# Thirteen of 64 gathered columns of an edge stage looked up by one-hot matmuls

## The reference

```
a_src = (h * att_src).sum(-1);  a_dst = (h * att_dst).sum(-1)
e     = leaky_relu(a_src[src] + a_dst[dst], 0.2)
ee    = exp(e - segment_max(e, dst)[dst])
agg   = segment_sum(h[src] * ee / segment_sum(ee, dst)[dst], dst)
```

## Time and profile before

| | us |
|---|---|
| median of 3 runs (10355.76 to 10371.48) | 10368.38 |
| profiled execution | 10367.71 |
| its span | 10366.0 |
| busy: PE / DVE / ACT / POOL | 4951.9 / 4237.3 / 2175.2 / 5594.5 |
| edge stage, from its first DMA to its last scan | 4590 to 9754 |

### The profile page before, as it was taken

One profiled execution on the slowest core, in us unless ns is written; L12 is line 12 of the kernel. 1 busy time (PEld: TensorE's weight loads), 2 busy tenths in 40 slices (PEclk: granted clock), 3 DMA queues, 4 the chain that ended last, 5 costly groups with the idle time before them and its releaser, 6 DMA issues. The chain is left out here.

```text
span 10366.0 us, 77502 instructions
## 1 busy us (share of the span) xinstructions
PE 4951.9 (48%) x21339; PEld 2907.9 (28%) x21339; DVE 4237.3 (41%) x9137; ACT 2175.2 (21%) x4107; POOL 5594.5 (54%) x5263
## 2 busy tenths in 40 slices
PE   6888888779955888841221112111221112111145
PEld 5555655557742344410010001000000001000011
DVE  5666566556669877731111111111111111111188
ACT  3443444323311222211111111111111111111000
POOL 2333333300013456357777777777777777777652
PEclk9898888889977999965565556655565556555577
DMA  2000000021110222231111111111111111111455
GB/s 91 34 28 33 25 24 25 22 85 61 57 63 25 55 52 53 38 73 35 37 40 35 34 35 39 38 35 34 38 40 34 35 36 38 39 34 35 69 181 186
DMA packets 388197, 510.48 MB, mean 49 GB/s; under 512 B 216517, under 2 KB 303358, under 8 KB 365442
## 3 DMA queue, kind: packets, MB, share of 16 engines
q1 hardware_dynamic: 191618, 258.32, 8.7%
q0 software_dynamic: 163968, 75.75, 6.5%
q10 hardware_dynamic: 32256, 171.98, 4.1%
HBM read 245.58 MB, written 263.86 MB: 49 GB/s over the span
## 5 line engine op out<-in xcount | busy, mean ns | idle before, releaser
L1665 POOL DMA_INDIRECT e_row<-rows_dram,e_idx x4096 | 3890.3, 950 | 1264.1 <-issue 1248.2
L1610 PE MATMUL e_bank<-e_hid,e_w 128*128 128x512 f32 x1024 | 592.6, 714 | 4050.7 <-ACT e_hid L1640 4050.7
L1698 DVE COPY e_idx<-e_allidx 128x64 int32 x64 | 13.6, 212 | 4205.1 <-DMA e_row<-rows_dram,e_idx 4205.1
L1610 PEld LDWEIGHTS e_bank<-e_hid,e_w 128*128 128x128 f32 x1024 | 220.8, 223 | 4353.7 <-issue 4353.7
L387 POOL COPY a_xc<-a_xp 128x1573 f32<-128x1573 f32 x104 | 400.3, 3853 | 679.5 <-PE a_bank L441 563.9
L1648 ACT ACTIVATE e_ex<-e_dx 128x512 f32<-128x512 f32 x64 | 38.5, 602 | 3418.1 <-DVEq L1711 3418.1
L1047 POOL DMA_INDIRECT c_yt<-yb_dram,keep_slots x256 | 384.6, 1502 | 580.3 <-DVE c_yg L1267 501.0
L396 POOL DMA_INDIRECT xb_dram<-a_so,a_sidx x256 | 251.9, 984 | 744.9 <-DVE a_sidx L669 416.8
L1603 PE MATMUL e_bank<-e_h,e_w 128*128 128x512 f32 x1024 | 509.8, 627 | 76.3 <-DMA e_h<-hn_dram 76.3
L199 DVE TENSOR_TENSOR a_cnta_hot<-a_cnta_iota,a_cnta_part 128x512 bf16<-128x512 bf16 x1184 | 518.0, 438 | 0.0
L1168 PE MATMUL c_conv<-c_xp,c_w 128*128 128x512 f32 x1152 | 513.7, 600 | 0.0
(11 more groups left out here) (353 smaller groups left out, 10090.5 us busy)
## 6 DMA issues: line engine op xcount, KB each, us to landing
e_row<-rows_dram,e_idx POOLq DMA_INDIRECT x4096
ys_dram<-e_y ACTq DMA_DIRECT2D x64, 1024.0 KB, 3.9
f_ye<-ys_dram SPq DMA_DIRECT2D x64, 1024.0 KB, 4.8
res_dram<-e_st ACTq DMA_DIRECT2D x64, 768.0 KB, 3.3
xb_dram<-a_taps SPq DMA_DIRECT2D x4, 5120.0 KB, 31.1
b_tok<-xb_dram SPq DMA_DIRECT2D x80, 256.0 KB, 2.6
yb_dram<-b_y ACTq DMA_DIRECT2D x80, 256.0 KB, 2.0
x_dram<-a_xs SPq DMA_DIRECT2D x9, 2048.0 KB, 6.3
```

The costliest lines, as they stand in the source:

```text
L1610: mm = nc.tensor.matmul(bank[UPB + n % DNB][:], w2[:, n % NE, f], hid[:, n % 2, f], start=(f == 0), stop=(f == NF1 - 1))
L1665: nc.gpsimd.indirect_dma_start(row[:, s, u], None, rows, bass.IndirectOffsetOnAxis(ap=idx[:, s, u:u + 1], axis=0)).then_inc(gath[s], 16)
```

## The change

Of each chunk's 64 columns POOL gathers the first 51 (UP); the other 13 (XG) are looked up by TensorE. A node index is split into a low part (10 bits: 8 groups g of 128) and a high part (5 bits: 32). The feature table of all nodes, 16 values each, lies in SBUF: partition l, group g, 32 x 16 values, 16 KB per partition. It is held as two pieces in float32r, a type of fewer mantissa bits: the rounded table, and what the rounding left; both products add in float32 in PSUM.

One look-up k (one column, 128 edges): PE multiplies a matrix whose columns all are the column's low codes with the identity, so that every partition has all 128 codes (`spread`); DVE compares them with 8 x 128 constants and gets 8 one-hot weights (`one_hot`); PE multiplies these with the 2 x 8 pieces and accumulates 16 matmuls of 512 columns into one bank (`found`): for each edge 32 candidates of 16 features; DVE multiplies them by a mask of the high code (`pick`) and sums over the 32. After 13 of them DVE computes the attention sums of these columns.

One-hots and `found` exist twice, `spread` once. DVE makes the one-hot of look-up k + 2 right after the product of look-up k. PE's order per chunk is look-ups 0 and 1, the experts, look-ups 2 to 12. ACT now does the experts of the next chunk before the exponentials of this one. `up` has two PSUM banks (the others go to `found` and `spread`). DVE waits for a stored state one use of the buffer later. The block before clears the first experts' semaphores on ACT. The indices have a semaphore of their own, so POOL doesn't wait for the weights; the table comes in by eight DMAs ahead of them on SP.

```diff
-    U = 64
+def edge_states(nc, passed, rows, srcs, cont, v, res, hn, ys, ident, att_src, w):
+
+
+    U, XG = 64, 13
+    UP = U - XG
     TURNS = FE // (2 * U)
-    UPB, DNB = 4, 2
+    CHUNKS = 2 * TURNS
+    UPB, DNB = 2, 2
+    HG, HS, PARTS = 8, NHI // 8, 2
...
+        codei = sb("codei", [P, 2, CHUNKS + 1, XG], I32)
+        code = sb("code", [P, 2, XG])
+        high = sb("high", [P, XG])
+        lowi, lows = sb("lowi", [P, HG], I32), sb("lows", [P, HG])
+        highi, highs = sb("highi", [P, HS], I32), sb("highs", [P, HS])
+        table = sb("table", [P, HG, HS, HF])
+        pieces = sb("pieces", [P, PARTS, HG, HS, HF], mybir.dt.float32r)
+        att = sb("att", [P, HF])
+        hot = sb("hot", [P, 2, HG, P], mybir.dt.float32r)
+        pick = sb("pick", [P, XG, HS])
+        prod = sb("prod", [P, 2, HS, HF])
+        aprod = sb("aprod", [P, XG, HF])
...
+        spread = ps("spread", [P, P])
+        found = [ps(f"found{z}", [P, HS, HF]) for z in range(2)]
+        bank = [ps(f"bank{i}", [P, NT]) for i in range(UPB + DNB)]
...
+        table_g = rows.rearrange("(s g l) c -> g l s c", g=HG, l=P)
...
-            sp.dma_start(allidx[:, 0:FE], srcs).then_inc(consts, 16)
+            sp.dma_start(allidx[:, 0:FE], srcs).then_inc(listed, 16)
+            for g in range(HG):
+                sp.dma_start(table[:, g], table_g[g][:, :, 0:HF]).then_inc(tabled, 16)
             for dst, src in ((w1[:], w["w1"].rearrange("e d f -> d e f")),
                              (w2[:], w["w2"].rearrange("e (f p) d -> p e f d", p=P)),
-                             (b1[:], w["b1"]), (b2[:], w["b2"])):
+                             (b1[:], w["b1"]), (b2[:], w["b2"]), (att[:], att_src.broadcast_to([P, HF]))):
...
+            def spread_code(k):
+                s, j = divmod(k % (2 * XG), XG)
+                nc.tensor.matmul(spread[:], code[:, s, j:j + 1].broadcast_to([P, P]), ident[:], start=True,
+                                 stop=True).then_inc(code_spread, 1)
+
             pe.wait_ge(consts, 80)
+            pe.wait_ge(coded, 1)
+            spread_code(0)
+            pe.wait_ge(pieced, 2 * PARTS - 1)
             with pe.Fori(0, TURNS) as i:
+                def look_up(k):
+                    pe.wait_ge(hot_ready, 2 * XG * i + (k + 1))
+                    spread_code(k + 1)
+                    pe.wait_ge(masked, 2 * XG * i + (k + 1))
+                    for g in range(HG):
+                        for q in range(PARTS):
+                            mm = nc.tensor.matmul(found[k % 2][:].rearrange("p s c -> p (s c)"), hot[:, k % 2, g],
+                                                  pieces[:, q, g].rearrange("p s c -> p (s c)"),
+                                                  start=(g == 0 and q == 0), stop=(g == HG - 1 and q == PARTS - 1))
+                    mm.then_inc(found_psum, 1)
...
-                up(0)
-                for n in range(TURN):
-                    if n + 1 < TURN:
-                        up(n + 1)
-                    down(n)
+                for s in range(2):
+                    for j in range(2):
+                        look_up(XG * s + j)
+                    up(STEP * s)
+                    for n in range(STEP * s, STEP * (s + 1)):
+                        if n + 1 < STEP * (s + 1):
+                            up(n + 1)
+                        down(n)
+                    for j in range(2, XG):
+                        look_up(XG * s + j)
+            pe.wait_ge(hot_ready, XG * CHUNKS + 1)
+            spread_code(1)
...
+            def experts_of(i, s):
...
+                outputs((s + 1) * STEP - 1)
+                act.wait_ge(y_ready, DNB + TURN * i + (s + 1) * STEP)
+                act.dma_start(ys[2 * i + s], y[:, s]).then_inc(y_stored[s], 16)
+
+            def states_of(i, s):
+                act.wait_ge(dx_ready, 2 * i + s + 1)
+                nc.scalar.activation(ex[:], dx[:], ACT.Exp)
+                nc.scalar.activation(weight[:], dx[:, 1], ACT.Exp).then_inc(ex_ready, 1)
+                act.wait_ge(st_ready, 2 * i + s + 1)
+                act.dma_start(res_c[2 * i + s], st[:, s]).then_inc(stored[s], 16)
+
+            experts_of(0, 0)
+            with act.Fori(0, TURNS - 1) as i:
+                experts_of(i, 1)
+                states_of(i, 0)
+                experts_of(i + 1, 0)
+                states_of(i, 1)
+            experts_of(TURNS - 1, 1)
             for s in range(2):
-                act.wait_ge(stored[s], 16 * TURNS)
+                states_of(TURNS - 1, s)
...
-                    for u in range(U):
+                    for u in range(UP):
...
+            dve.wait_ge(listed, 16)
+            for s in range(2):
+                nc.vector.tensor_copy(idx[:, s], allidx[:, s * U:s * U + UP]).then_inc(idx_ready, 1)
+            looked_up = allidx[:, 0:FE].rearrange("p (n u) -> p n u", u=U)[:, :, UP:]
+            nc.vector.tensor_scalar(codei[:, 0, 0:CHUNKS], looked_up, HG * P - 1, None, ALU.bitwise_and)
+            nc.vector.tensor_scalar(codei[:, 1, 0:CHUNKS], looked_up, (HG * P).bit_length() - 1, None,
+                                    ALU.logical_shift_right).then_inc(init, 1)
+            dve.wait_ge(made, 2)
+            nc.vector.tensor_copy(lows[:], lowi[:])
+            nc.vector.tensor_copy(highs[:], highi[:])
+            dve.wait_ge(init, 2)
+            nc.vector.tensor_copy(code[:, 0], codei[:, 0, 0]).then_inc(coded, 1)
+            dve.wait_ge(coded, 1)
             dve.wait_ge(consts, 80)
-            for s in range(2):
-                nc.vector.tensor_copy(idx[:, s], allidx[:, s * U:(s + 1) * U]).then_inc(idx_ready, 1)
-            dve.wait_ge(init, 1)
-            K = 13
+
+            def one_hot(k, first):
+                dve.wait_ge(code_spread, first + (k + 1))
+                nc.vector.tensor_tensor(hot[:, k % 2], spread[:].unsqueeze(1).broadcast_to([P, HG, P]),
+                                        lows[:].unsqueeze(2).broadcast_to([P, HG, P]), ALU.is_equal
+                                        ).then_inc(hot_ready, 1)
+
+            one_hot(0, 0)
+            dve.wait_ge(tabled, 16 * HG)
+            for q in range(PARTS):
+                nc.vector.tensor_copy(pieces[:, q], table[:]).then_inc(pieced, 1)
+                if q < PARTS - 1:
+                    dve.wait_ge(pieced, 2 * q + 1)
+                    nc.vector.tensor_tensor(table[:], table[:], pieces[:, q], ALU.subtract).then_inc(pieced, 1)
+                    dve.wait_ge(pieced, 2 * q + 2)
+            one_hot(1, 0)
+            K = 18
             with dve.Fori(0, TURNS) as i:
                 for s in range(2):
                     n = 2 * i + s
                     link = Chain(dve, chain, K * n)
+                    link(nc.vector.tensor_copy(code[:, 1 - s], codei[:, 0, bass.ds(n + 1, 1)].rearrange(
+                        "p n u -> p (n u)")))
+                    link(nc.vector.tensor_copy(high[:], codei[:, 1, bass.ds(n, 1)].rearrange("p n u -> p (n u)")))
+                    link(nc.vector.tensor_tensor(pick[:], highs[:].unsqueeze(1).broadcast_to([P, XG, HS]),
+                                                 high[:].unsqueeze(2).broadcast_to([P, XG, HS]), ALU.is_equal))
+                    for j in range(XG):
+                        k = XG * s + j
+                        dve.wait_ge(found_psum, 2 * XG * i + (k + 1))
+                        nc.vector.tensor_tensor(prod[:, k % 2], found[k % 2][:],
+                                                pick[:, j].unsqueeze(2).broadcast_to([P, HS, HF]), ALU.mult
+                                                ).then_inc(masked, 1)
+                        one_hot(k + 2, 2 * XG * i)
+                        dve.wait_ge(masked, 2 * XG * i + (k + 3))
+                        nc.vector.tensor_reduce(row[:, s, UP + j, 0:HF], prod[:, k % 2].rearrange("p s c -> p c s"),
+                                                AX.X, ALU.add).then_inc(picked, 1)
+                    dve.wait_ge(picked, 2 * XG * i + XG * (s + 1))
+                    link(nc.vector.tensor_tensor(aprod[:], row[:, s, UP:, 0:HF],
+                                                 att[:].unsqueeze(1).broadcast_to([P, XG, HF]), ALU.mult))
+                    link(nc.vector.tensor_reduce(row[:, s, UP:, HF:],
+                                                 aprod[:].rearrange("p u (h e) -> p u h e", e=NE), AX.X, ALU.add))
...
-                    dve.wait_ge(gath[s], 16 * U * i + 16 * U)
-
-                    nc.vector.tensor_copy(idx[:, s], allidx[:, bass.ds((2 * i + s + 2) * U, U)]
+                    dve.wait_ge(gath[s], 16 * UP * i + 16 * UP)
+
+                    nc.vector.tensor_copy(idx[:, s], allidx[:, bass.ds((2 * i + s + 2) * U, UP)]
...
+                    dve.wait_ge(stored[s], 16 * i + 16)
...
-                for s in range(2):
-                    dve.wait_ge(stored[s], 16 * i + 16)
```

More of the change, by code:

```diff
@@ L1487, in _ @@
             sp.wait_ge(fixed, 16)
+        @block.scalar
+        def _(act):
```

(38 more changed lines are left out.)

22 lines of the change are left out of this document (14 added, 8 removed).

## The result

The changed kernel takes 10,502.5 us (median of 4 runs, 10,498.3 to 10,504.6) against 10,369.4 (median of 4 runs): by the ratio of the means 1.0131 times as long, 95% interval 1.0113 to 1.0148. The forecast was 10,235, faster; its sign was wrong. The profiled execution took 10,503.91 us, its span 10,502.1.

A forecast was written before the change was run, and what follows sets the result against it. GpSimd's gathers were taken to set the 80.3 us chunk period. Afterwards a loop through four engines sums to 77.6 us; 63 periods plus start and end give 133 us less, 10,235 us, range 10,050 to 10,620.

The forecast's parts named there:

- the price of one matmul: TensorE's look-up: a 512-column float32r matmul takes 0.214 us, the lower end of 0.214 to 0.857.
- T: Edge stage: the period of one chunk, 80.3 us before the change and forecast at 77.6 after it.
- The experts and the order of waits: Edge stage: experts 13.85 us; then exponentials, states and the other 11 look-ups follow one another, once per chunk.
- The pause: TensorE stands still once per chunk during exponentials, states and the next one-hot: 13.3 us.
- the slow clock: TensorE restarts at the lower of two clock levels after standing still, costing 2.45 us per chunk.
- hand-overs: Edge stage: waits not visible in a row, 0.3 us per chunk, bounds 0 and 2.
- The terms of the start: Edge stage: constants at 47 us, preparation, two cold look-ups, experts, eleven look-ups; first chunk's last look-up 124 us in.
- The turning point: Edge stage: the gain is gone at a period of 79.7 us, 10 ns more for each of 208 matmuls.
- C: Look-ups: VectorE sets the pace (10,610 us) or hand-overs are longer (10,340); with other periods of 80 to 85, chance 0.17.
- B: Look-up matmuls: float32r moves at half the rate, 0.429 us each, time 13,100 us; chance 0.11.
- A: Edge stage: GpSimd's gathers stay the bound at 64.0 us per chunk, time 9,323 us; chance 0.07.
- D: TensorE keeps its clock through the pause: 75.2 us per chunk, 10,080 us; chance included in the forecast's 0.58.

## Why the prediction was wrong

*The step that failed* is the price of one matmul: "float32r keeps fewer bits than float32 (hence two pieces), so it needs no second half-word pass and lies nearest to the bf16 row. The look-up is 0.24 + 16 x 0.214 = 3.66 us, and 13 are 47.6." The second pass is indeed gone (13,312 records for as many matmuls), but a float32r matmul takes 0.2333 us, not 0.214. The look-up is 3.96 us, thirteen are 51.5. That is 3.9 us per chunk and 245 of the 269 us by which the profiled execution missed; the kernel with two bf16 pieces, which has the forecast's look-up, has the forecast's time.

*The other terms of T.* The experts and the order of waits came as forecast. The pause is 13.54 (forecast 13.3), the slow clock 2.77 (2.45), what is left for hand-overs 0.24 (0.3). DVE needs 0.691 + 1.214 + 1.020 = 2.93 us a look-up (3.25) and waits 1.2 in each in the mean. The constants landed at 4631, 39 us in (47); the first chunk's last look-up was done at 4712.3 (4714), and the other 63 took 81.85 each: 9868.8. (The terms of the start add up to 123 us, not to the 124 used.)

*The turning point* was named: the gain gone at 10 ns a matmul more. It was 19 ns more. But the step took the lower end of 0.214 to 0.857 for a type of which the earlier trace rows held none, and gave all that lay above it 0.28: 0.17 to "C or another T", of which only C, slower DVE or hand-overs, was worked out, and 0.11 to B. B had the right point and the wrong mechanism (half the rate would have been 0.429). With 2.1 us of margin over 208 matmuls of an unmeasured kind, 0.65 for faster was too much. That 10,502 lies within the stated range is luck: the range reached that high for C, and C's causes were not there.

*The rivals.* A did not occur, for the reason given (ACT's order); the kernel with the states moved shows that it is DVE's wait for the exponentials, which this order makes late, and comes to 9,470. There PE's 65.4 lies just above POOL's 64.0, so at 3.96 a look-up A's pace was out of reach in any order. B's rate is refuted: a float32r matmul moves 4 bytes per partition each 0.456 ns. The Trainium skill's "SBUF — State Buffer" (section "A bandwidth-pool intuition that's wrong (but worth ruling out)") gives the moving operand 2 B a lane at 2.4 GHz, a figure that it states for bf16; float32r exceeds it here 1.8 times, so it is no limit for this type. C is refuted: DVE's 2.93 us and the 0.24 of hand-overs both stayed under the forecast. D fell: the first look-up after the pause shows a granted clock of 0.55.

The Trainium skill's "TensorE: Matmul & The Clock Gate" (section "Back-to-back issue gap") gives N / 2.4 + 2.5 ns as the gap of single matmuls, 215.8 ns at 512 columns, and about 131 ns for a stream of weight loads and matmuls, without regard to type. The bf16 streams here (0.2157 us) agree with the former and not with the latter; float32r agrees with neither (0.2333 at 512 columns; at 256 0.1138 or 0.1178, against 109.2 ns by the formula).

## What to carry to other kernels

When a loop's margin is divided by the number of instructions in it and comes out at a few per cent of one, measure that instruction in its own type and shape before trusting the sum: "about as fast as bf16" was 8% short. When two engines hand work to each other once per period, write the period as a sum around the loop and not as the largest busy time; here every term of the sum but one came within 0.4 us, and moving the one wait that it named a chunk later took 1,033 us off, where three columns fewer in the look-up took 817. And when two engines are near balance, count which of them starts earlier: a lead of 41 us was gone only after twelve chunks.

## What the runs showed of the hardware

- float32r matmuls of 512 columns start 0.2333 us apart, of 256 columns 0.1178 or 0.1138, by stretches of a chunk: 0.44 to 0.46 ns a column; bf16 0.2157 for 512, 0.42 ns. With 64 weight columns instead of 128 it hardly changes (3.92 us against 3.96 for sixteen and the spread). What sets the rate is open.
- Weight loads took 0.187 us for 128 columns of float32r, 0.134 for 64, 0.098 for 128 of bf16; loads of 0.187 did not hold up matmuls 0.1178 or 0.1138 us apart.
- After 13 us without a matmul the first look-up of the changed kernel took from 5.4 to 6.9 us in place of 3.96, differently from chunk to chunk; in the kernel that kept PE busy, after 2.0 to 2.7 us of idling, 4.06 (39 chunks) or 5.6 (24).
